# All one-bank PSUM jobs in the idle value bank, keys staged in four parts, down products two steps later

## The reference

```python
x = x + tanh(g_xattn[0]) * xattn(layernorm(x), ctx, ctx)
x = x + tanh(g_ffn[0]) * ffn(layernorm(x), w_gate, w_up, w_down, ...)
```

## Time and profile before

| what | value |
|---|---|
| median of 3 runs | 1081.37 us (1081.37 to 1084.7) |
| the profiled execution, its own time | 1085.51 us |
| its span | 1083.8 us |
| PE busy | 954.7 us, 88% |
| DVE busy | 846.4 us, 78% |
| ACT busy | 685.4 us, 63% |
| POOL busy | 311.7 us, 29% |

### The profile page before, as it was taken

The page is one execution under the profiler, slowest core; times in us unless marked ns, Lnnn a source line. Parts: engine busy times, 40 slices in busy tenths (PEclk is TensorE's granted clock), DMA queues, the critical chain, the costliest instruction groups (busy, mean ns, idle before and its releaser), DMA issues.

```text
span 1083.8 us, 21067 instructions
## 1 busy us (share of the span) xinstructions
PE 954.7 (88%) x7706; PEld 393.8 (36%) x7706; DVE 846.4 (78%) x1418; ACT 685.4 (63%) x1388; POOL 311.7 (29%) x335
## 2 busy tenths in 40 slices
PE   3588798999999999999989999999989998898575
PEld 2223233333333434343433333343434343343342
DVE  7777789898887888777777879687877888635886
ACT  2146567776776766767666767676666766766543
POOL 3011333333221413231322324141323233334232
PEclk9999999999999999999999999999999999999777
DMA  7971333232792221123932221216822020000001
GB/s 148 130 213 58 87 103 77 57 92 55 168 114 61 70 58 44 43 60 91 136 67 54 60 69 31 69 34 133 122 49 61 4 54 26 1 11 1 11 2 39
DMA packets 157231, 74.89 MB, mean 69 GB/s; under 512 B 111096, under 2 KB 142920, under 8 KB 157128
## 3 DMA queue, kind: packets, MB, share of 16 engines
q1 hardware_dynamic: 155240, 67.70, 29.4%
q0 software_dynamic: 1760, 5.77, 1.9%
q10 hardware_dynamic: 128, 0.07, 0.0%
HBM read 43.28 MB, written 4.19 MB: 44 GB/s over the span
## 4 chain that ended last, share of the span: by engine, by line
PE 44%; DVE 39%; issue 8%; ACT 5%; POOL 3%; DMA 0%; SPq 0%; DVEq 0%; ACTq 0%; POOLq 0%
DVE mch L1181 18%; PE ps L951 13%; PE ps L925 8%; PE ps L972 6%; PE ps L868 6%; PE ps L995 3%; DVE ff L1088 3%; PE ps L873 2%; DVE ff L1084 2%; ACT pr L686 1%; DVE upd L1224 1%; DVE hmax L1277 1%; DVE ff L1081 1%; POOL t_T L467 1%; DVE ff L1271 1%
## 5 line engine op out<-in xcount | busy, mean ns | idle before, releaser
L686 ACT ACTIVATE pr<-ps 128x512 f32<-128x512 f32 (+4 forms) x832 | 397.5, 531 | 186.1 <-PE ps L925 97.9
L1181 DVE TENSOR_REDUCE mch<-ps 128x2 f32<-128x1024 f32 (+4 forms) x416 | 431.7, 1055 | 46.2 <-PE ps L868 21.6
L951 PE MATMUL ps<-pr,vf 128*33 128x512 f32 (+4 forms) x1664 | 380.2, 537 | 0.0
L925 PE MATMUL ps<-qst,kst 97*64 97x512 f16 (+4 forms) x1600 | 251.0, 369 | 9.4 <-ACT pr L686 6.6
L868 PE MATMUL ps<-kTh,qTh 32*128 32x512 f16 (+4 forms) x832 | 155.1, 370 | 52.4 <-DVE mch L1181 36.7
L868 PEld LDWEIGHTS ps<-kTh,qTh 32*128 32x128 f16 x832 | 39.4, 91 | 263.2 <-DVE mch L1181 103.2
L925 PEld LDWEIGHTS ps<-qst,kst 97*64 97x64 f16 (+1 forms) x1600 | 77.4, 110 | 103.5 <-ACT pr L686 69.9
L951 PEld LDWEIGHTS ps<-pr,vf 128*33 128x33 f32 (+1 forms) x1664 | 86.0, 112 | 55.4 <-issue 2.3
L1263 DVE SCALAR_TENSOR_TENSOR ff<-ps,scs,wsb 128x352 f32<-128x352 f32 x56 | 32.4, 582 | 53.7 <-PE ps L972 53.7
L972 PE MATMUL ps<-wgu,t_T 128*64 128x352 bf16 x768 | 65.3, 312 | 0.0
L1172 DVE TENSOR_TENSOR kTl<-ps,kTh 128x1024 f16<-128x1024 f32 (+1 forms) x32 | 31.6, 992 | 42.9 <-ACT kTh L642 42.9
(11 more groups left out here) (156 smaller groups left out, 1194.0 us busy)
## 6 DMA issues: line engine op xcount, KB each, us to landing
kst<-kTh SPq DMA_DIRECT2D x128, 100.1 KB, 2.2
ksrc<-in_ctx SPq DMA_DIRECT2D x16, 768.0 KB
vf<-in_ctx SPq DMA_DIRECT2D x48, 256.0 KB, 5.6
kst<-kTl SPq DMA_DIRECT2D x64, 100.1 KB, 2.3
xs<-in_x SPq DMA_DIRECT2D x16, 256.0 KB, 4.1
qst<-qTh SPq DMA_DIRECT2D x128, 32.0 KB, 1.9
near<-in_ctx SPq DMA_DIRECT2D x4, 1024.0 KB, 7.7
out<-xs SPq DMA_DIRECT2D x16, 256.0 KB, 2.0
```

The costliest lines, as they stand in the source:

```text
L686: nc.scalar.activation(pr[0:kn, n % NP, q0:S], ps[0:kn, j, q0:S], ACT.Exp, scale=SCALE).then_inc(ex_done, 1)
L925: last = nc.tensor.matmul(ps[a:e, j, q0:S], kst[s][0:ST, r, k0 + a:k0 + e], qst[s][0:ST, r, q0:S], start=True, stop=(t < DT))
L951: nc.tensor.matmul(ps[64 * j:64 * j + VW, 2 + pp % 2, q0:S], vf[0:kn, t, h, :], pr[0:kn, n % NP, q0:S], start=(t == 0), stop=(t == NT - 1) ...
L1181: nc.vector.tensor_reduce(mch[:, qt, 2 * hp:2 * hp + 2, c], both[:, :, 0:k1 - k0], AX.X, ALU.max).then_inc(dve_free, 1)
```

## The change

1. A one-bank job always takes the idle value bank if there is one; the condition of two steps between jobs (`spare_at`) is gone.
2. The keys are staged in four parts of at most 512 columns (512, 512, 512, 65) at u = 6, 10, 12 and 13 instead of two, and each, fitting one bank, goes into the idle value bank.
3. The down product of tiles 0 to 8 is two steps later, at u = 16, since at u = 14 there is no idle bank (`down_at`).
4. A weight job (from 4 on) that would fall in the last step of a pair is two steps later and one that would fall in the first is one step later (`weight_turn_at`): weights 6 and 23 by two, 13 and 20 by one.

```diff
-    STAGE_AT, ... = {10: 1, 13: 2, 19: 0}, ...
+    STAGE_AT, ... = {6: 1, 10: 2, 12: 3, 13: 4, 19: 0}, ...
-    PARTS = (1, 2, 0)
+    PARTS = (1, 2, 3, 4, 0)
...
+    def down_at(n):
+        return DOWN_AT + 2 if n < TAIL - 3 else DOWN_AT
...
     def weight_turn_at(j):
-        return weight_base(j) + (6 if j < DC else 4)
+        at = weight_base(j) + (6 if j < DC else 4)
+        return at + {NT - 1: 2, 0: 1}.get((at - LAG) % NT, 0) if j >= DC else at
...
     def fits_one_bank(job):
-        return job[0] in ("turn", "suf", "shift", "rows", "down") or job[0] == "stage" and job[2] == 0 or job[0] == "weight" and job[1] >= DC
+        return job[0] in ("turn", "suf", "shift", "rows", "down", "stage") or job[0] == "weight" and job[1] >= DC
...
         one = spare_bank(at) if at is not None and fits_one_bank(job) else None
-        if one is not None and at - spare_at.get(one, -9) >= 2:
+        if one is not None:
             banks[job], spare[job] = one, min((at - LAG) // NT, GALL * PAIRS - 1)
-            spare_at[one] = at
...
         def stage_cols(part):
-            return ((0, S), (0, K_CUT), (K_CUT, SK))[part]
+            return (0, S) if part == 0 else (512 * (part - 1), min(512 * part, SK))
```

More of the change, by code:

```diff
@@ L48, in flamingo_gated_block @@
     SPB = NG * STEPS
-    K_CUT = 8 * P
     HALVES = ((0, P // 2), (P // 2, P))
@@ L80, in flamingo_gated_block @@
     TAIL = TILES - QT
-    TILE_STEPS, TILE_PERIOD = 27, 22
+    TILE_STEPS, TILE_PERIOD = 28, 22
     END = LAST + 8
@@ L129, in flamingo_gated_block @@
     banks, before_in_bank, latest, dve_count, act_count = {}, {}, {}, {}, {}
-    spare, spare_at, before_values, slots = {}, {}, {}, []
+    spare, before_values, slots = {}, {}, []
     def fits_one_bank(job):
-        return job[0] in ("turn", "suf", "shift", "rows", "down") or job[0] == "stage" and job[2] == 0 or job[0] == "weight" and job[1] >= DC
+        return job[0] in ("turn", "suf", "shift", "rows", "down", "stage") or job[0] == "weight" and job[1] >= DC
     def spare_bank(at):
@@ L189, in flamingo_gated_block @@
                 numbered("hidden", n, at=at)
-            if k == DOWN_AT:
+            if k == down_at(n):
                 numbered("down", n, at=at)
@@ L358, in load_keys @@
             if gg >= 1:
-                sp.wait_ge(st_mm, 3 * gg - 1)
+                sp.wait_ge(st_mm, len(PARTS) * gg - 1)
             cols = slice(g * P, (g + 1) * P)
@@ L632, in stage_cols @@
         def stage_cols(part):
-            return ((0, S), (0, K_CUT), (K_CUT, SK))[part]
+            return (0, S) if part == 0 else (512 * (part - 1), min(512 * part, SK))
         def stage_high(act, gg, part):
             c0, c1 = stage_cols(part)
-            act.wait_ge(st_mm, 3 * gg + PARTS.index(part) + 1)
+            act.wait_ge(st_mm, len(PARTS) * gg + PARTS.index(part) + 1)
             if gg >= 2 and part == PARTS[0]:
@@ L640, in stage_high @@
                     act.wait_ge(stk[gg % 2][r], (gg // 2) * STK)
-            to = (qTh, kTh, kTh)[part]
+            to = qTh if part == 0 else kTh
             nc.scalar.copy(to[:, gg % 2, c0:c1], slot(("stage", gg, part))[:, 0:c1 - c0]).then_inc(hi_done, 1)
@@ L648, in norm_cols @@
             if gg >= 1:
-                act.wait_ge(st_mm, 3 * gg)
+                act.wait_ge(st_mm, len(PARTS) * gg)
             for qt in tiles:
@@ L755, in _ @@
             norm_cols(act, 0, range(QT))
-            stage_high(act, 0, 2)
-            stage_high(act, 0, 0)
+            for part in PARTS[1:]:
+                stage_high(act, 0, part)
             norm_cols(act, 1, range(QT))
@@ L862, in max_turn @@
             if j == 0:
-                pe.wait_ge(hi_done, 3 * gg + 3)
+                pe.wait_ge(hi_done, len(PARTS) * (gg + 1))
             d0 = NEAR + P * qt
@@ L1169, in stage_low @@
             c0, c1 = stage_cols(part)
-            dve.wait_ge(hi_done, 3 * gg + PARTS.index(part) + 1)
-            hi, lo = ((qTh, qTl), (kTh, kTl), (kTh, kTl))[part]
+            dve.wait_ge(hi_done, len(PARTS) * gg + PARTS.index(part) + 1)
+            hi, lo = (qTh, qTl) if part == 0 else (kTh, kTl)
             nc.vector.tensor_tensor(lo[:, gg % 2, c0:c1], slot(("stage", gg, part))[:, 0:c1 - c0], hi[:, gg % 2, c0:c1],
```

2 lines of the change are left out of this document (1 added, 1 removed).

## The result

The changed kernel takes 1090.35 us (median of 13 runs, 1088.34 to 1091.3) where the kernel before takes 1083.12 in as many runs beside it (1080.75 to 1088.09). The ratio is 1.0055, with a 95% interval of 1.0042 to 1.0067: slower by 4.5 to 7.3 us. The forecast stood on the scale of the first three runs (1081.4), where the ratio gives 1087.3.

The account below looks back on a forecast made before the run. PE, busy 88% of the span, was taken as the bound. Prologue 1.9, group 0 0, groups 1 to 4 5.5, groups 5 to 13 -6.1 and clock 0 gave 1081.4 + 1.3 = 1082.7 us, range 1074 to 1090.

Parts of the forecast that it names:

- the even case: Whole kernel: the summed terms, 1.3 us more, 1082.7 us, within 3.2 us of no change; chance 0.38.
- Prologue: Key parts and queries alternate over two slots: 1.5 us later in group 0, 0.4 in group 1, together 1.9 us slower.
- In group 1, without the columns between, it is 0.4: Staging of group 1: without ACT's four normalised columns between, the two-slot chain costs 0.4 us instead of group 0's 1.5.
- Groups 1 to 4, waits: New waits at weights 17.2 us, 11.7 given back: 5.5 us slower; ends 0, or 12.9 if only 4.3 is given back.
- The clock: Whole kernel: low-clock stretches of 1.5 us each, two may go, two may come; counted as 0, 3 us either side.
- Groups 5 to 13: Max and hidden-copy waits against new turn waits behind the down product, summed over the nine groups: 6.1 us less.
- the gains at u = 10 and u = 21: Groups 5 to 13: PE's max waits go, 0.60 us at u = 10 and 0.96 at u = 21 (1.60 in groups 5, 9).
- I count nothing for it: Groups 5 to 13, u = 13: the 0.70 us hidden-copy wait goes, but exponentials wait behind the same copies; gain taken as nothing.
- most of this comes back at u = 11 to 13: Groups 8 and 12: DVE stays late, so most of the 1.97 us wait at u = 10 returns; 0.7 us gained each.
- Slower by ACT's copies: Groups 1 to 4: turn, stage and suf jobs wait as priced, POOL's waits stay; 4.7 to 7.7 us slower, chance 0.20.
- The freed slots bring nothing: Nine groups keep 0.96 us at u = 21 because DVE is late and pay 0.98; 10.8 us slower, 1092.2, chance 0.13.
- the faster case: Groups 1 to 4 even, new waits falling where PE would have waited for DVE or POOL; -7.2 us, 1074.2, chance 0.29.

Follow-up runs that it names:

- the fill experiment: Changed kernel plus eleven extra 512-column matmuls, results overwritten, before each turn behind weights 6 and 23; ratio 1.0008 to the kernel before, against 1.0055 for the change.

## Why the prediction was right in its range and wrong in its middle

The likeliest case, even, did not come. On the scale of the forecast the result is 1087.3 us: inside 1074 to 1090, outside the even case's own 1078 to 1085, and on the side to which 0.33 had been given. That it lies inside is in part luck: groups 1 to 4 lost 7.6 us more than forecast, 13.1 against a worst case of 12.9, and groups 5 to 13 gained 5.7 us more, and the two errors nearly cancel.

- **Prologue (+1.9, measured +3.1).** Group 0 came out as worked: the first max job at 18.77 us for 18.7. The step "In group 1, without the columns between, it is 0.4" failed: it is 1.5. The columns are not what makes the chain slow. Without them the third part still waits for PE, ACT's copy and DVE's remainder of the first, and the queries for those of the third, 1.33 and 1.30 us, where one wait of 1.41 stood before.
- **Group 0 (0, measured +0.7).** Idle time fell by 2.5 us and the clock took 3.2: the profile has the stretch at 0.90 where it was 0.95. Kernels with one order there differ by as much, so the 3.2 us are not shown to be the change's.
- **Groups 1 to 4, waits (+5.5, measured +4.2 of idle time).** Term by term it holds. New waits: 14.0 us behind a weight (7.4 + 1.9 + 1.8 + 1.1 + 0.9 + 0.9) for 15.1 (9.0 + 1.3 + 4.8), with the two long ones 2.53 and 2.15 for 2.6 and 2.2. Waits of weights behind a job of the same step: 3.4 us for 2.1 (1.9 and 1.0 in two places and small ones, not seven of 0.3). Given back: max waits 4.3 to 0.7, the keys' remainder 5.3 to 0.5, POOL 7.7 to 2.8 (t_T and t_q together), 13.3 us for 11.7.
- **The clock (0 with 3 to either side; measured +8.9 in groups 1 to 4 and +8.8 over the kernel).** This is the step that failed: "Two may go with the waits of groups 8 and 12, two may come with those of weights 6 and 23. I count nothing". The two of groups 8 and 12 did go (-1.2 us). Those that came cost more than 1.5 us each, and there was one more: the two holds cost 4.7 us of clock by the fill experiment, and the stretch of 10 us in group 3 stands behind a new wait of 1.94 us at a weight, for which the forecast had 0.3. That this third one hangs on its wait is argued, not shown: it goes with the wait in the kernels with the weights put back, but it was not filled alone. The forecast took 1.5 us for such a stretch from a row in which one group of values was 0.5 us longer; here a fall lasts 7 us and slows every matmul in it.
- **Groups 5 to 13 (-6.1, measured -11.8).** The turn waits behind the down product were right (eight of 0.97 us for 0.98), and so were the gains at u = 10 and u = 21. Two steps failed. "I count nothing for it" at u = 13: nine waits for the hidden copies, 6.3 us, went, and 2.3 us for exponentials came, so 4.0 us stay gained (groups 6, 7, 10 and 11 are 0.9 us shorter for 0.6, groups 5 and 9 1.8 for 1.2). And in groups 8 and 12 "most of this comes back at u = 11 to 13": it did not. Each is 2.5 us shorter, where 0.7 was taken; the wait of 1.97 us went whole, with no lasting lag of DVE behind it. Group 13 lost 0.6 us where nothing was forecast, its rows and its turn waiting 1.0 and 0.7 us.
- **The rivals.** "Slower by ACT's copies" gives the right size, 4.7 to 7.7 us, for a reason that did not hold: POOL's waits did not stay but fell by 4.9 us. Its condition, groups 1 to 4 losing more than 7.4 us, was met by the clock. "The freed slots bring nothing" is refuted by 17.6 us of max waits falling to 2.4. That PE would have waited anyway in groups 1 to 4 (the faster case) is refuted by its idle time growing.
- **The Trainium skill.** The Trainium skill's rule that independent matmul groups should rotate through PSUM banks (Perfetto Trace Analysis, Optimizing Tensor Performance) agrees with the turn waits of both stretches: 7.4 and 8.5 us, gone but for 0.7 in the kernels that separate the jobs. By the Trainium skill's fixed cost for each instruction on DVE (Perfetto Trace Analysis, Optimizing Scalar/DVE Operations) the prediction had an estimate of 4 us for the four key parts. DVE's remainders of the keys do take more in sum, 36.3 us (32.7 + 3.6) for 31.8; but the kernel with weights and down products as before, in which the four parts remain, is 1.7% faster, so they were no burden on the whole.
- **The signs.** As forecast: max waits in groups 5 to 13 under 5 us (2.4), hidden copies gone, 0.3 us a group for exponentials, nine turn waits of 0.7 to 1 us, eleven short waits behind weights in groups 1 to 4 (three turns, three key stages, two suf, two shift, one query stage) and two of over 2 us, first max job at 18.7. Wrong: nothing among the signs asked for the clock, though PE's busy time at an unchanged count of matmuls was the clearest one.

## What to carry to other kernels

When a bank is shared, ask for every pair of neighbours in it how much of PE's own work lies between them, and who reads the first: here the same idle bank saved 20 us in the middle groups (513 us instead of 533) and lost 17 where jobs stood next to a weight, the clock included, and 10 where a turn followed a down product. The kernels that keep only those pairs apart beat both the kernel before (two steps between all jobs) and the change (none). How much of the 20 us comes from staging the keys in one-bank parts and how much from the lifted rule is not shown: no kernel ran with the four parts under the old rule. And price an added wait on PE twice, once for itself and once for the clock after it; in the profile compare PE's busy time at an equal count of instructions before looking for waits.

## What the runs showed of the hardware

- After an idle time of PE the granted clock can fall for several microseconds: 2.53 us idle at 169.7 us, then matmuls at the lower level from 172.24 to 179.30. Eleven matmuls in this hold and eleven in that of 2.15 us, whose results nobody reads, kept the clock up behind both and made the kernel 0.5% faster.
- The fall is not certain. The same 2.53 us in the kernel with the weights' part alone was followed by full speed (the 2.15 us were not). In group 13 two waits of 0.9 to 1.0 and 0.72 us were followed by slow matmuls in five kernels and by none in the four others. What decides is open; it was not tried apart.
- So PE's busy time can differ where the order does not: 87.1 to 90.8 us up to group 1 in three kernels with one order there. In groups 1 to 4 it repeated, 210.1 to 210.3 us in four kernels and 219.5 in two. A difference of a few microseconds between two profiled executions is the edit's only where it repeats.
